# A graph layer on one core: x loaded as one run a lane with 16 lanes ahead, weights fetched once and doubled by TensorE, the last nodes' counts in one packet

## What is computed

```python
h = maximum(layernorm(x), 0)                     # per node, over 64 features
neighbors = (adj @ h) / (num_neighbors[:, None] + 1e-7)
out = relu(concatenate([h, neighbors], -1) @ fc_w.T + fc_b)
return x + out
```

## Time and profile before

| what | value |
|---|---|
| time, median of 3 runs | 247.53 us (247.29 to 247.62) |
| the profiled execution, its own time | 247.57 us |
| its span, first to last instruction | 245.8 us |
| mean DMA rate over the span | 418 GB/s |
| PE busy | 207.6 us (84%) |
| DVE busy | 41.3 us (17%) |
| ACT busy | 15.2 us (6%) |

### The profile page before, as it was taken

How to read it: one execution, slowest core, us unless ns; L and a number is a source line. 1 busy time by engine, 2 the same in 40 slices (tenths; PEclk the granted TensorE clock), 3 DMA queues, 4 the chain that set the end, 5 groups by cost and what they waited for, 6 DMA issues and landing times.

```text
span 245.8 us, 2444 instructions
## 1 busy us (share of the span) xinstructions
PE 207.6 (84%) x1084; PEld 86.0 (35%) x1084; DVE 41.3 (17%) x101; ACT 15.2 (6%) x35; POOL 4.2 (2%) x14
## 2 busy tenths in 40 slices
PE   0268689997879987999899899799997699798995
PEld 0143224342324433443344243234332233133662
DVE  1762033304300200050000530221000000002401
ACT  2130011201200110010000400000000000000000
POOL 6000000000000000000000000000000000000000
PEclk9999979999979999979999999899999999999999
DMA  9899999999999999999999999999999999999995
GB/s 305 381 440 447 440 441 424 427 427 435 414 433 428 433 423 427 427 427 422 443 440 427 427 424 423 432 437 437 424 432 427 411 427 424 421 420 418 424 403 211
DMA packets 7109, 102.79 MB, mean 418 GB/s; under 512 B 1364, under 2 KB 2172, under 8 KB 3900
## 3 DMA queue, kind: packets, MB, share of 16 engines
q1 hardware_dynamic: 6400, 102.37, 98.0%
q10 hardware_dynamic: 700, 0.28, 0.4%
HBM read 101.37 MB, written 1.28 MB: 418 GB/s over the span
## 4 chain that ended last, share of the span: by engine, by line
DMA 63%; PE 33%; SPq 2%; issue 0%; DVE 0%
DMA raw<-adj_group 63%; PE acc L612 28%; PE acc L631 2%; PE y L577 2%; PE turned L612 1%; SPq L249 1%; SPq L262 1%; PE y L646 0%; SPq L253 0%; PE y L644 0%; PE turned L565 0%; DVE out_sb L527 0%; PE acc L660 0%; SPq L258 0%; DVE sums L510 0%
## 5 line engine op out<-in xcount | busy, mean ns | idle before, releaser
L612 PE MATMUL acc<-raw,g_sb 128*64 128x512 f32 (+1 forms) x780 | 162.0, 570 | 21.5 <-DMA raw<-adj_group 21.5
L612 PEld LDWEIGHTS acc<-raw,g_sb 128*64 128x64 f32 x780 | 56.5, 141 | 121.8 <-issue 87.8
L612 PE MATMUL turned<-raw,g_sb 128*64 128x196 f32 x156 | 15.1, 336 | 1.3 <-DMA raw<-adj_group 1.1
L443 DVE TENSOR_TENSOR out_sb<-y,bias 128x128 f32<-128x128 f32 x20 | 4.4, 284 | 51.2 <-ACT g_sb L355 51.2
L577 PE MATMUL y<-w_both,ht 128*128 128x256 f32 (+1 forms) x40 | 12.1, 441 | 0.8 <-ACT ht L349 0.8
L612 PEld LDWEIGHTS turned<-raw,g_sb 128*64 128x64 f32 x156 | 10.2, 136 | 6.4 <-DMA raw<-adj_group 4.8
L493 DVE TENSOR_TENSOR sums<-acc,rnn_bc 128x512 f32<-128x512 f32 x4 | 2.6, 686 | 58.2 <-PE acc L612 56.2
L577 PEld LDWEIGHTS y<-w_both,ht 128*128 128x128 f32 x40 | 8.0, 217 | 3.9 <-issue 2.7
L519 DVE TENSOR_TENSOR out_sb<-y,out_sb 128x512 f32<-128x512 f32 (+1 forms) x5 | 3.2, 638 | 25.7 <-PE y L644 22.5
L565 PE MATMUL turned<-ident,h_pairs 128*128 128x128 f32 x20 | 3.7, 315 | 4.4 <-DVE h_pairs L431 4.4
L419 DVE TENSOR_REDUCE var<-sums 128x8 f32<-128x512 f32 x5 | 3.4, 687 | 21.5 <-ACT sums L329 21.5
(11 more groups left out here) (57 smaller groups left out, 44.9 us busy)
## 6 DMA issues: line engine op xcount, KB each, us to landing
raw<-adj_group SPq DMA_DIRECT2D x9, 5120.0 KB, 26.9
raw<-adj_group SPq DMA_DIRECT2D x7, 4096.0 KB, 28.4
raw<-adj_group SPq DMA_DIRECT2D x4, 2048.0 KB, 28.7
raw<-adj_group SPq DMA_DIRECT2D x7, 784.0 KB, 24.8
raw<-adj_group SPq DMA_DIRECT2D x1, 3840.0 KB, 24.4
raw<-adj_group SPq DMA_DIRECT2D x3, 1024.0 KB, 26.7
raw<-adj_group SPq DMA_DIRECT2D x4, 392.0 KB, 20.2
x_sb<-x SPq DMA_DIRECT2D x2, 576.0 KB, 4.7
```

The costliest lines, as they stand in the source:

```text
L443: last = nc.vector.tensor_tensor(to[:, 2 * k:2 * k + 2, :], weighed_parts(k, 0)[:, :, s, :], bias[:].unsqueeze(1).to_broadcast([LANES, 2, ...
L612: last = nc.tensor.matmul(acc[b][s * HALF:(s + 1) * HALF, 0:width], g_sb[:, t, :], raw[:, c + c0:c + c0 + width], start=g < G - 1 and t == ...
```

## The change

SP now issues x on lanes 0 to 15 first and on lanes 16 to 127 second, each lane's 36 nodes as one run of 9,216 bytes. It issues the weights once, into `w_rows`, a piece of `rnn_diag[1]` that is free until `expand(1)`, without a wait. PE multiplies them by the identity twice, into the two halves of PSUM bank `y[0]`, and ACT copies the two halves into `w_both`. The last 392 counts go to one lane as one run (`rnn_last`, in lane 0 of `ht_rows`); DVE inverts them there, with a row each for the addition and the reciprocal, and PE spreads them with a matmul of one row of ones. Their diagonal (L472) and the clearing of `nn` (L390) are gone, and L510 reads `rnn_bc` with a step of two.

```diff
-        nn = sb("nn", [LANES, TILES])
-        rnn = sb("rnn", [LANES, TILES])
+        nn = sb("nn", [LANES, ROWS])
+        rnn = sb("rnn", [LANES, ROWS])
+        rnn_last = ht_rows[0:1, :]
+        w_rows = rnn_diag[1][0:F, 0, 0:2 * F]
...
-            def load_x(k):
-                r = slice(ROWS // 2 * k, ROWS // 2 * (k + 1))
-                sp.dma_start(x_sb[:, r, :], x[0:TAIL0, :].rearrange("(p r) f -> p r f", r=ROWS)[:, r, :]
+            for lanes in (slice(0, ENGINES), slice(ENGINES, LANES)):
+                sp.dma_start(flat(x_sb[lanes, 0:ROWS, :]), x[0:TAIL0, :].rearrange("(p r) f -> p (r f)", r=ROWS)[lanes]
                              ).then_inc(x_loaded[0], 16)
...
-            sp.wait_ge(weights_cleared, 1)
-            for s in range(2):
-                k = slice(s * F, (s + 1) * F)
-                sp.dma_start(w_both[k, s, :].rearrange("r (k c) -> r k c", k=2), fc_t.rearrange("(k r) c -> r k c", k=2)
-                             ).then_inc(weights_loaded, 16)
+            sp.dma_start(w_rows.rearrange("r (k c) -> r k c", k=2), fc_t.rearrange("(k r) c -> r k c", k=2)).then_inc(weights_loaded, 16)
...
-                act.wait_ge(nn_cleared, 1)
-                act.dma_start(nn[:, 0:ROWS], num_neighbors[0:TAIL0].rearrange("(p r) -> p r", r=ROWS)
+                act.dma_start(nn[:], num_neighbors[0:TAIL0].rearrange("(p r) -> p r", r=ROWS)
                               ).then_inc(nn_loaded, 16)
-                act.dma_start(nn[0:LAST_LANES, ROWS:TILES].rearrange("p (s i) -> p s i", s=2),
-                              num_neighbors[TAIL0:N].rearrange("(s p i) -> p s i", s=2, i=2)).then_inc(nn_loaded, 16)
+                act.dma_start(rnn_last, num_neighbors[TAIL0:N].rearrange("(a c) -> a c", a=1)).then_inc(nn_loaded, 16)
...
+            act.wait_ge(weights_cleared, 1)
+            act.wait_ge(weights_doubled, 1)
+            for s in range(2):
+                k = slice(s * F, (s + 1) * F)
+                nc.scalar.activation(flat(w_both[k, s:s + 1, :]), y[0][k, 0:2 * F], ACT.Copy).then_inc(weights_copied, 1)
             for b in range(SETS):
                 ln_square(b)
...
-                dve.wait_ge(rnn_chain, 1)
+                nc.vector.tensor_scalar(rnn_last, rnn_last, DIV_EPS, None, ALU.add).then_inc(rnn_chain, 1)
+                dve.wait_ge(rnn_chain, 2)
                 nc.vector.reciprocal(rnn[:], nn[:]).then_inc(rnn_chain, 1)
+                nc.vector.reciprocal(rnn_last, rnn_last).then_inc(rnn_chain, 1)
...
-                    c, r = slice(0, BLOCK), rnn_diag[b % 2][:, s, :]
+                    c, o, r = slice(0, BLOCK), ones[:, 0:HALF], rnn_diag[b % 2][:, s, :]
                     if b == ALONE:
                         c = slice(BLOCK // 2, BLOCK // 2 + SIDE)
-                        r = rnn_diag[b % 2][:, 1, s * SIDE:(s + 1) * SIDE]
+                        o, r = ones[0:1, 0:HALF], rnn_last[:, s * SIDE:(s + 1) * SIDE]
...
             pe.wait_ge(ident_ready, 1)
+            pe.wait_ge(weights_loaded, 16)
+            for s in range(2):
+                last = nc.tensor.matmul(y[0][s * HALF:(s + 1) * HALF, 0:2 * F], ident[0:F, 0:F], w_rows, start=True,
+                                        stop=True, tile_position=(0, s * HALF))
+            last.then_inc(weights_doubled, 1)
             turn(0)
-            pe.wait_ge(weights_loaded, 32)
+            pe.wait_ge(weights_copied, 2)
             weigh(0)
```

More of the change, by code:

```diff
@@ L13 @@
 LANES = 128
+ENGINES = 16
 BLOCK = 512
@@ L159, in gnn_layer @@
         x_loaded = [sem("x_loaded_main"), sem("x_loaded_last")]
-        nn_cleared = sem("nn_cleared")
         nn_loaded = sem("nn_loaded")
@@ L163, in gnn_layer @@
         weights_loaded = sem("weights_loaded")
+        weights_doubled = sem("weights_doubled")
+        weights_copied = sem("weights_copied")
         bias_cleared = sem("bias_cleared")
@@ L249, in load @@
                 sp.dma_start(raw[:, place(n):place_end(n)], rows[:, i0 * w:i1 * w]).then_inc(loaded(n)[0], 16)
-            def load_x(k):
-                r = slice(ROWS // 2 * k, ROWS // 2 * (k + 1))
-                sp.dma_start(x_sb[:, r, :], x[0:TAIL0, :].rearrange("(p r) f -> p r f", r=ROWS)[:, r, :]
+            for lanes in (slice(0, ENGINES), slice(ENGINES, LANES)):
+                sp.dma_start(flat(x_sb[lanes, 0:ROWS, :]), x[0:TAIL0, :].rearrange("(p r) f -> p (r f)", r=ROWS)[lanes]
                              ).then_inc(x_loaded[0], 16)
-            load_x(0)
-            load_x(1)
             sp.dma_start(tail(x_sb)[0:PAD0], tail_nodes(x)[0:PAD0]).then_inc(x_loaded[1], 16)
-            sp.wait_ge(weights_cleared, 1)
-            for s in range(2):
-                k = slice(s * F, (s + 1) * F)
-                sp.dma_start(w_both[k, s, :].rearrange("r (k c) -> r k c", k=2), fc_t.rearrange("(k r) c -> r k c", k=2)
-                             ).then_inc(weights_loaded, 16)
+            sp.dma_start(w_rows.rearrange("r (k c) -> r k c", k=2), fc_t.rearrange("(k r) c -> r k c", k=2)).then_inc(weights_loaded, 16)
             for n in range(len(LOADS)):
@@ L389, in _ @@
             nc.vector.memset(w_both[:], 0.0).then_inc(weights_cleared, 1)
-            nc.vector.memset(nn[:], 1.0).then_inc(nn_cleared, 1)
             def parts(b):
@@ L449, in invert_neighbors @@
                 nc.vector.tensor_scalar(nn[:], nn[:], DIV_EPS, None, ALU.add).then_inc(rnn_chain, 1)
-                dve.wait_ge(rnn_chain, 1)
+                nc.vector.tensor_scalar(rnn_last, rnn_last, DIV_EPS, None, ALU.add).then_inc(rnn_chain, 1)
+                dve.wait_ge(rnn_chain, 2)
                 nc.vector.reciprocal(rnn[:], nn[:]).then_inc(rnn_chain, 1)
+                nc.vector.reciprocal(rnn_last, rnn_last).then_inc(rnn_chain, 1)
             def expand(b):
-                dve.wait_ge(rnn_chain, 2)
+                dve.wait_ge(rnn_chain, 4)
                 if b >= 2:
@@ L468, in expand @@
                     shape = [LANES, RUN, F]
[L469 to L474, removed]
+                    last = nc.vector.tensor_tensor(split(to[:, 0, 0:BLOCK // 2]), ident_twice[:].unsqueeze(1).to_broadcast(shape),
+                                                   rnn[:, m:ROWS:FULL].unsqueeze(2).to_broadcast(shape), ALU.mult)
                 last.then_inc(diag_ready, 1)
@@ L511, in scale_last @@
                                             tile_major(acc[LAST][:, 0:SIDE], 2)[:, i, :],
-                                            rnn_bc[:, ALONE, BLOCK // 2 + i * LAST_LANES:BLOCK // 2 + (i + 1) * LAST_LANES],
+                                            tile_major(rnn_bc[:, ALONE, BLOCK // 2:BLOCK // 2 + SIDE], 2)[:, i, :],
                                             ALU.mult).then_inc(scaled, 1)
@@ L597, in spread @@
                     k = slice(s * HALF, (s + 1) * HALF)
-                    c, r = slice(0, BLOCK), rnn_diag[b % 2][:, s, :]
+                    c, o, r = slice(0, BLOCK), ones[:, 0:HALF], rnn_diag[b % 2][:, s, :]
                     if b == ALONE:
                         c = slice(BLOCK // 2, BLOCK // 2 + SIDE)
-                        r = rnn_diag[b % 2][:, 1, s * SIDE:(s + 1) * SIDE]
-                    last = nc.tensor.matmul(y[b % 2][k, c], ones[:, 0:HALF], r, start=True, stop=True,
-                                            tile_position=(0, s * HALF))
+                        o, r = ones[0:1, 0:HALF], rnn_last[:, s * SIDE:(s + 1) * SIDE]
+                    last = nc.tensor.matmul(y[b % 2][k, c], o, r, start=True, stop=True, tile_position=(0, s * HALF))
                 last.then_inc(spread_done, 1)
```

## The result

| | before | after |
|---|---|---|
| time, median of 6 runs each | 247.41 us | 248.49 us (248.4 to 248.6) |
| ratio | | 1.0044, interval 1.0034 to 1.0054 |
| span, median | 245.6 us | 246.3 us |
| time outside the span, median | 1.80 us | 2.18 us |
| DVE busy, profiled execution | 41.3 us | 43.3 us |

What follows compares the result with a forecast made beforehand. It took the DMA engines' work ahead of the last load as the bound. Gains of 0.06 + 0.15 + 0.12 + 0.34 + 0.1 = 0.77 us from 247.57 gave 246.8 us, range 246.3 to 247.8.

Steps and rivals of the forecast that it cites:

- What bounds the kernel: DMA stream: the engines' work ahead of the last load sets the time; removed work gains its engine time over 16.
- Prices of packets: DMA packets saved: x as one run a lane 0.06 us, weights once 0.15, last counts 0.12.
- The start: First DMA microseconds: 16 lanes first give every engine an early packet, gaining 0.34 us, plus 0.1 for late engines.
- The rival of the door: x's first packets: neighbouring lanes share a way into SBUF and queue; +0.7 us, 248.3 us; chance 0.14.
- TensorE doubles the weights, ACT copies: ACT's wait and copies ahead of the first square: covered by a margin of 1.5 us, cost 0.
- DVE on one lane: Reciprocal of the last 392 counts on one lane: 2.6 us within DVE's idle time, cost 0.
- L510 with a step of two: Strided read on the path after the last load: taken as 0, at most 0.1 us.

Runs made afterwards that it cites:

- 112 lanes first: Changed kernel with x's two issues the other way round, lanes 0 to 111 and then lanes 112 to 127: 249.44 us.
- 64 and 64: Changed kernel with x in two issues of 64 lanes each, four lanes to an engine: 249.95 us.
- eight times 16: Changed kernel with x in eight issues of 16 neighbouring lanes each: 252.65 us.
- the whole x: Changed kernel with x in one issue over all 128 lanes, one run of 9,216 B a lane: 247.47 us.
- the changed kernel with x as before: Changed kernel with x loaded as two halves of 18 nodes on all lanes, weights and counts still changed: 247.51 us.
- the version with the whole x: Changed kernel with x in one issue over 128 lanes and ACT's program two instructions shorter, by moves to SP and PE: 247.14 us.

## Why the prediction was wrong

**What bounds the kernel**: right. What the loading of x lost was there again at the end. In the three kernels with the largest losses (112 lanes first, 64 and 64, eight times 16) DVE began on x at 8.44, 9.01 and 11.39 us, 1.9, 2.5 and 4.9 us later than before, and the spans are 1.7, 2.2 and 4.9 us longer, with 0.2 to 0.3 us of packets saved in each. The time from the last load's landing to the last row on DVE was 2.96 to 3.00 us in the kernel before and in every one that loads x otherwise.

**Prices of packets** (0.06, 0.15 and 0.12 us): right in sum. The spans show -0.1 for the counts, another -0.1 for the weights, and -0.1 for one run a lane (245.3 against 245.4), as far as a tenth can be read; 0.3 where 0.33 was forecast. (The store's 28 ns is a mean over all 210 packets; if the other 14 are marks of 9 ns, the 196 of 512 B took 30, which moves the weights' term by under 0.01 us.)

**The start** (0.34 + 0.1 us): this is the step that failed, and the larger part of the error. Its first half was right: with 16 lanes ahead all engines had a packet by 2.2 us, and these took 425 ns. What I didn't price is the pace of what comes after. I took x's later packets at 179 ns for 4,608 B from the earlier trace rows and doubled the bytes, although the row holds for issues over all 128 lanes only. Split into 16 and 112 lanes, the same bytes took 471 ns a packet, against 355 with the whole x. Seven packets an engine at 116 ns more are 0.8 us. Against the changed kernel with x as before, x's part cost 0.9 us of span, where the sum had it as a gain of 0.5 (0.06 + 0.34 + 0.1). The sign I had named for a won start, more bytes before 2.9 us, came true in a kernel that lost.

**The rival of the door** had the right sign and, as far as the lanes' runs show, the right mechanism, but the wrong place: it looked for the crowd in the first 16 packets and dismissed the 112 lanes as "some tenths more", and it got 0.14. That its +0.7 us is also what the span grew by is luck, since its price was for first packets of 1.4 us and these took 0.43. The first packets weren't slow by their own records. The 13 packets of x that begin in 2.2:2.55 us were: with nine end marks they hold 228.9% of 5.6 us.

```profile
q1 hardware_dynamic: 22, 0.12, 228.9%
```

That is 0.98 us each. It looks like the backlog of the 16 lanes, but a slow packet stands near the start without them too. With the whole x in one issue, the packets before 2.2 us are these nine, at 1.15 us each:

```profile
q1 hardware_dynamic: 9, 0.08, 29.3%
```

By 3.1 us both kernels have begun 34 packets of x, which hold 22.0 us in the changed kernel and 19.9 us with the whole x. That is 0.13 us an engine. The 92 packets behind them hold 10.7 us more than at 355 ns, 0.67 us an engine. So most of the loss is in the 112 lanes' own pace, and why an early packet takes a microsecond stays open. The sign by which the rival was to be known ("above 1.2 us by the door" for the first packets) would have cleared it wrongly. The Trainium skill's rule on ports in "SBUF — State Buffer", Door 1, was the better guide here than my doubt of it (64 lanes at 220 GB/s agree with it). I held it against full pace in the earlier trace rows, which didn't bear on it, as the text itself says.

**TensorE doubles the weights, ACT copies** (cost 0): right in the span, where the stream still waits for the load. Wrong outside it: 0.37 us that no term of the sum had, from three instructions in ACT's program. The prediction counted what an added instruction delays and not that a longer ACT program can cost time by itself. No row of the profile before could have shown that; the time outside the span, 1.8 us, stood in the table and was taken as fixed.

**DVE on one lane** (2.6 us, nobody waiting): right.

```profile
L455 DVE RECIPROCAL ht_rows<-ht_rows 1x392 f32<-1x392 f32 x1 | 2.5, 2532 | 0.0
...
L451 DVE TENSOR_SCALAR nn<-nn 128x36 f32<-128x36 f32 x1 | 0.2, 174 | 0.0
```

The wait of 1.9 us for the counts is gone, and was worth nothing. **L510 with a step of two**: 0.27 us in the chain as before, right.

Together: 0.9 (x) - 0.1 - 0.1 in the span and 0.37 outside make 1.07, and 1.08 was measured. The forecast was a gain of 0.77. x's part was off by 1.4 us of that difference, the time outside by 0.37, and the packets of weights and counts by under 0.1.

## What to carry to other kernels

A load over all 128 lanes ran at full pace; cut by lanes, the same packets crowded while every DMA engine read as busy. So keep the lanes whole, cut along the rows instead, and read GB/s beside the share. A row's price for a packet holds for the set of lanes it was taken with. When a change adds instructions, compare time less span as well as the span: an ACT program three instructions longer cost more here (0.37 us) than all the packet savings together brought (0.3).

## What the runs showed of the hardware

- Packets of 9,216 B into SBUF took 355 ns with one issue over 128 lanes, 471 ns with 16 and then 112 lanes, 486 to 645 ns with 112 and then 16. The rates in 3.1 to 4.9 us were 430, 220 and 140 GB/s for issues of 128, 64 and 16 lanes.
- Early packets of 9,216 B took 425 ns (the first of each engine, 16 lanes ahead), 0.98 us (those behind them) and 1.15 us (the first nine with the whole x).
- Three more ACT instructions that wait for nothing raised the time outside the span from 1.80 to 2.16 us, one more left it at 1.80; four semaphores and three matmuls did nothing. What happens in that time stays open.
- DMA time lost in the first microseconds reached the end, to within 0.3 us (x 1.9, 2.5 and 4.9 us later, spans 1.7, 2.2 and 4.9 us longer). The last load landed 0.46 us later in the changed kernel, the span's median is 0.7 us longer, and the version with the whole x landed it 0.35 us earlier than the kernel before.
